# State space block: 192 channels as 128 rows and 64 on both row halves, projections before the running sums, turned x before the small network

## What is computed

```
h      = _ln(x)                                   # 192 channels
zxbcdt = h @ in_proj_w.T                          # z: 384, xBC: 512, dt: 6 columns
xBC    = silu(conv4(xBC) + conv_b)                # xs 384, B 64, C 64
dt     = softplus(dt + dt_bias);  dA = exp(-dt * exp(A_log))
hn     = hprev * dA_t + dtx_t * B_t;  y_t = hn . C_t     # 6 heads of 64, 64 states
y      = rmsnorm((y + D_skip * xs) * silu(z)) * ssm_norm_w
x      = x + y @ out_proj_w.T
f      = _ln(x) @ fc1_w.T                         # 768 columns: a (384) and g (384)
return x + (f_a * silu(f_g)) @ fc2_w.T            # "the small network"
```

## Time and profile before

| what | us |
|---|---|
| median of 3 runs (2194.4 to 2195.69) | 2195.28 |
| the profiled execution | 2192.55 |
| its span | 2190.8 |
| TensorE busy, of the span | 1974.5 (90%) |
| VectorE, ScalarE, GpSimd busy | 1137.2, 750.8, 428.5 |
| first turned rows y of the state space block | 932.84 |
| first `new_state` (start of full turn 0) | 975.01 |
| `new_state` of turns 1, 3, 4 | 1033.52, 1142.61, 1196.30 |
| `new_state` of turn 7 | 1357.98 |
| last write of h in the block | 1405.45 |

### The profile page before, as it was taken

How to read it: one execution, slowest core, us unless ns; L and a number is a source line. 1 busy time by engine, 2 the same in 40 slices (tenths; PEclk the granted TensorE clock), 3 DMA queues, 4 the chain that set the end, 5 groups by cost and what they waited for, 6 DMA issues and landing times. The chain is left out here.

```text
span 2190.8 us, 27883 instructions
## 1 busy us (share of the span) xinstructions
PE 1974.5 (90%) x10040; PEld 1243.3 (57%) x10048; DVE 1137.2 (52%) x2687; ACT 750.8 (34%) x1251; POOL 428.5 (20%) x526
## 2 busy tenths in 40 slices
PE   4996618999999999679999999699999999999997
PEld 2343513444444444446666665465567888888886
DVE  5798577666666756156677676337411222222221
ACT  1434002555455545355555554121111111111111
POOL 5200100121012201211111111110371222322232
PEclk9988558999999999979999999789999999999999
DMA  2600002121111111000000000200123221222221
GB/s 64 229 34 0 0 13 89 47 61 52 51 37 58 51 51 30 13 14 6 6 6 6 6 6 6 97 2 1 48 77 95 67 59 30 67 60 61 67 36 19
DMA packets 68618, 94.30 MB, mean 43 GB/s; under 512 B 15354, under 2 KB 57630, under 8 KB 66209
## 3 DMA queue, kind: packets, MB, share of 16 engines
q1 hardware_dynamic: 52354, 76.76, 10.9%
q0 software_dynamic: 16128, 15.76, 4.1%
HBM read 54.53 MB, written 39.47 MB: 43 GB/s over the span
## 5 line engine op out<-in xcount | busy, mean ns | idle before, releaser
L972 DVE TENSOR_REDUCE row_max<-c_ps_m 128x1 f32<-128x512 f32 x384 | 252.6, 686 | 115.9 <-PE c_ps_m L1130 110.5
L1308 ACT ACTIVATE e<-c_ps_s 128x512 f32<-128x512 f32 x384 | 216.6, 596 | 222.1 <-PE c_ps_s L1146 221.3
L2593 DVE TENSOR_TENSOR e_f<-e_ps_u,e_gate 128x512 f32<-128x512 f32 x120 | 83.0, 691 | 271.2 <-ACT e_gate L2875 178.7
L2394 POOL DMA_INDIRECT out<-m_o,m_row_of x80 | 125.7, 1571 | 281.5 <-issue 251.6
L2810 PE MATMUL e_ps_o<-m_w,e_f 128*128 128x192 f32 x960 | 162.6, 326 | 0.9 <-DVE e_f L2593 0.9
L1130 PE MATMUL c_ps_m<-c_kT,qT 96*128 96x512 bf16 x384 | 150.3, 398 | 11.0 <-DVE row_max L972 10.9
L2810 PEld LDWEIGHTS e_ps_o<-m_w,e_f 128*128 128x128 f32 x960 | 158.1, 190 | 3.3 <-DVE e_f L2593 1.3
L1146 PE MATMUL c_ps_s<-qT,c_kT 97*128 97x512 bf16 x384 | 145.5, 389 | 12.3 <-ACT e L1308 5.0
L2875 ACT ACTIVATE e_gate<-e_ps_g 128x512 f32<-128x512 f32 x120 | 71.6, 597 | 242.3 <-PE e_ps_g L2784 162.3
L2778 PE MATMUL e_ps_g<-m_xT,m_w 128*128 128x256 f32 x480 | 129.6, 392 | 1.0 <-DVE h L2425 1.0
L2778 PE MATMUL e_ps_u<-m_xT,m_w 128*128 128x256 f32 x480 | 123.2, 379 | 0.0
(11 more groups left out here) (430 smaller groups left out, 3766.2 us busy)
## 6 DMA issues: line engine op xcount, KB each, us to landing
dealt<-x SPq DMA_DIRECT2D x8, 1290.0 KB, 15.1
m_x<-dealt SPq DMA_DIRECT2D x40, 258.0 KB, 2.7
spread<-parts SPq DMA_DIRECT2D x24, 384.0 KB, 2.4
qT<-spread SPq DMA_DIRECT2D x144, 64.0 KB, 2.4
c_kT<-spread SPq DMA_DIRECT2D x144, 64.0 KB, 2.4
m_w<-in_w13e SPq DMA_DIRECT2D x8, 1152.0 KB, 5.3
m_w<-in_w2e SPq DMA_DIRECT2D x8, 576.0 KB, 6.4
out<-h SPq DMA_DIRECT2D x8, 384.0 KB, 4.5
```

The costliest lines, as they stand in the source:

```text
L972: dve.tensor_reduce(row_max[:, n // J, n % J:n % J + 1], ps_m[:, n % 2, :], AX_X, ALU.max)\
L1308: act.activation(e[:, n % LIVE_E, :], ps_s[:, n % 2, :], ACT.Exp, scale=QSCALE).then_inc(e_ready, 1)
L2394: pool.indirect_dma_start(out=out_rows, out_offset=bass.IndirectOffsetOnAxis(ap=row_of[:, n % 2, r:r + 1], axis=0), in_=o[:, n % 2, r, :], ...
```

## The change

1. The 192 channels stand as rows 0 to 127, and the last 64 channels twice, on rows 0 to 63 and on rows 64 to 127. For this `y` and `y2` are 256 columns wide; VectorE copies columns 128 to 191 to 192 to 255 after a drain (`tensor_copy`, at the end of `apply_1` and of `apply_2`), and the turned rows are two blocks of 128 rows. The weights `wz`, `wx`, `wf1` and `ln12` are laid out the same way (`halves`).
2. `projections(*keys)` takes the place of `steps`, `project` and `hidden`. It runs the 128-row matmul of each key first, and then the 64-row matmuls of all keys, in turn on the lower and the upper row half.
3. The order of products: dt, x0, x1, z0 ahead of `chunk`; x2, x3, z1, z2 ahead of `running_sums`; turned x 0 and 1 ahead of the small network, 2 and 3 after its first pair. `ssm_order` has the same order, which also changes which product stands five places ahead of which.
4. ScalarE: all three `z_silu` directly after `conv_silu` 0; `conv_silu` 1 to 3 after the squares and ahead of `decay`.
5. VectorE: `times_cb` 0 between `norm_2` and `apply_2`; `times_dt` 0 and 1, `times_cb` 1 and `norm_1` behind `apply_2`; `times_cb` 2 and 3 and `times_c` at the end. The addition of x2 to h goes to GpSimd, and VectorE waits for it (`x2_added`) at `add_out` of the next sequence and at `add_o`.
6. GpSimd: `rstd_1` of t + 2 after two of the four `dtx_rest`. In `apply_1` y is now given free only after both y and xm are written, and copied.

```diff
-        begin(("dt", 0), ("x", 0), ("x", 1), ("x", 2), ("x", 3), ("z", 0), ("sums", 0))
+        begin(("dt", 0), ("x", 0), ("x", 1), ("z", 0), ("x", 2), ("x", 3), ("z", 1), ("z", 2), ("sums", 0))
...
+            def projections(*keys):
+
+                for key in keys:
+                    k, t, i = key
...
+                    free(key)
...
+                        w, col, rows = weights(key)
+                        pe.matmul(bank(key), w[:, 0, col:col + P], rows[:, 0, :], start=True, stop=False)
+                for n, key in enumerate(keys):
+                    half = row_half[n % 2]
...
+                        w, col, rows = weights(key)
+                        last = pe.matmul(bank(key), w[half, 1, col:col + P], rows[half, 1, :], start=False, stop=True)
+                    last.then_inc(w_psum, 1)
...
                     norm_2(t)
+                if begins:
+                    times_cb(u, 0)
+                if ends:
+                    apply_2(t)
...
                     conv_silu(u, 0)
-                    z_silu(u, 0)
+                    for m in range(KD):
+                        z_silu(u, m)
                 if ends:
                     for j in range(J):
                         squares(t, j)
                 if begins:
+                    for i in range(1, 4):
+                        conv_silu(u, i)
                     decay(u)
...
+                    here = kit.h[:, t * J:(t + 1) * J, :]
+                    pool.tensor_tensor(here, here, x2[:, :, :], ALU.add).then_inc(x2_added, 1)
```

More of the change, by code:

```diff
@@ L1715, in apply_2 @@
                 dve.wait_ge(r2_ready, t + 1)
[L1716 to L1720, removed]
+                ln_apply(dve, y2[:, :, 0:C], x2, mv2, rstd2)
+                dve.drain()
+                dve.tensor_copy(y2[:, :, C:2 * P], y2[:, :, P:C]).then_inc(y2_ready, 1)
             def times_gate(t, m):
@@ L1761, in turn @@
                     norm_2(t)
+                if begins:
+                    times_cb(u, 0)
+                if ends:
+                    apply_2(t)
+                if begins:
+                    times_dt(u, 0)
+                    times_dt(u, 1)
+                    times_cb(u, 1)
                 if later:
@@ L1764, in turn @@
                 if ends:
-                    apply_2(t)
-                    add_x2(t)
+                    times_gate(t, 0)
                 if begins:
-                    for j in range(J):
-                        times_cb(u, j)
+                    times_dt(u, 2)
+                    times_dt(u, 3)
+                if later:
+                    apply_1(t + 2)
+                if ends:
+                    times_gate(t, 1)
+                    times_gate(t, 2)
+                if begins:
+                    times_cb(u, 2)
+                    times_cb(u, 3)
                     for j in range(J - 1):
                         times_c(u, j)
[L1772 to L1779, removed]
                 if ends:
@@ L1819, in turn_rows @@
                 for j in range(J):
-                    last = pe.transpose(bank(key)[0:CH, j * P:(j + 1) * P], src[:, j, c * CH:(c + 1) * CH],
-                                        kit.ident[:, :])
+                    last = pe.transpose(bank(key)[:, j * P:(j + 1) * P], src[:, j, c * P:(c + 1) * P], kit.ident[:, :])
                 last.then_inc(w_psum, 1)
[L1824 to L1828, removed]
-                    for c in range(2):
-                        last = pe.matmul(bank(key)[:, j * NH:(j + 1) * NH], yT[:, c, j * P:(j + 1) * P], wz[:, c, DI:ZW],
-                                         start=c == 0, stop=c == 1)
-                last.then_inc(w_psum, 1)
@@ L1834, in project, with weights @@
-            def project(k, t, i):
-                key = (k, t, i)
-                w, m = (wx, XORDER[i]) if k == "x" else (wz, i)
-                free(key)
-                for c in range(2):
-                    last = pe.matmul(bank(key), w[:, c, m * P:(m + 1) * P], yT[:, c, :], start=c == 0, stop=c == 1)
-                last.then_inc(w_psum, 1)
+            row_half = (slice(0, P // 2), slice(P // 2, P))
+            def weights(key):
+                k, t, i = key
+                if k in ("g", "a"):
+                    return wf1, (KD + i if k == "g" else i) * P, y2T
+                return (wx, XORDER[i] * P, yT) if k == "x" else (wz, i * P, yT)
@@ L1965, in output @@
                 last.then_inc(w_psum, 1)
-            def hidden(k, t, m):
-                key = (k, t, m)
-                if k == "g" and m == 0:
-                    pe.wait_ge(by_act["y2"], count("y2", t, 1))
-                free(key)
-                col = (KD + m if k == "g" else m) * P
-                for c in range(2):
-                    last = pe.matmul(bank(key), wf1[:, c, col:col + P], y2T[:, c, :], start=c == 0, stop=c == 1)
-                last.then_inc(w_psum, 1)
             def turn(t):
```

104 lines of the change are left out of this document (55 added, 49 removed).

## The result

The changed kernel takes 2240.94 us (median of 4 runs, 2238.66 to 2243.26); the kernel before, run beside it, takes 2194.84 (2189.66 to 2195.69). The ratio is 1.0216, with a 95% interval of 1.0203 to 1.0229: slower by 46 us. The span of the profiled execution went from 2190.8 to 2240.7.

What follows compares the result with a forecast made beforehand. With TensorE nearly saturated, the new order makes the loop across engines bind: 58.0 us plus 2.0 for the clock a turn. Turns +37.0, prologue +10.7, tail -0.9 on 2192.55, plus 2.7 to the median: 2242 us, 8-in-10 range 2210 to 2265.

Steps and rivals of the forecast that it cites:

- The wait at the sums: In each turn TensorE stands still 4.1 us ahead of the running sums, until ScalarE's silu of z0.
- the band of 2 to 3: In each turn TensorE waits 2 to 3 us ahead of y2.
- Tables: ScalarE's two exposed table switches a turn: only the 1.28 us load counted; the skill page gave some 19 us more.
- The clock: In each full turn, half clock behind TensorE's waits costs 2.0 us, bounds 0 to 5.
- The clock falls twice: Rival: clock falls twice a turn, stays down through the small network, 5 us a turn, 2263 us; chance 0.16.
- the rival at 2228: Rival: the clock stays full through the turns, 14 us less, 2228 us; chance 0.20.
- Work saved: Row halves at 0.48 us a pair cut TensorE's work by 4.2 us a turn, from 52.0 to 47.8.
- dt's halves: Ahead of the end of chunk: dt's halves might run beside x0's, then 0.9 us less.
- stays the bound: Rival: TensorE stays the bound and the kernel gets faster, turns of 49.5 us, 2169 us; chance 0.10.
- The conv silus: ScalarE's silu of conv 3 (0.65), load and decay (about 2.0) now come ahead of the rows, on the loop.
- Prologue and tail: Before the first new_state: sums 4.3 us later, 6.4 more behind them, +10.7 together; tail in turn 7, -0.9.
- The sum: Seven turns +37.0 us, prologue +10.7, tail -0.9: +46.8 on the profiled execution of 2192.55 us.

Runs made afterwards that it cites:

- e2: Changed kernel with x2 in the first group of projections and z0 in the second: 2217.97 us, ratio 1.0116 to the kernel before.
- e3: Changed kernel with VectorE's first times_cb behind apply_2 again: 2226.22 us, ratio 1.0153 to the kernel before.
- e10: Changed kernel with both x2 in the first group instead of z0 and times_cb 0 behind apply_2: 2247.72 us, ratio 1.0037 to the kernel before.
- e4: Changed kernel with unread matmuls filling two TensorE waits, four ahead of the sums and two ahead of y2: 2222.87 us, ratio 1.0128 to the kernel before.
- e5: Changed kernel with all 64-row matmuls on the lower row half: 2295.58 us, ratio 1.033 to the kernel before.
- e9: e8 with the first gate's product and first two dt products ahead of apply_1 on VectorE: 2215.68 us, ratio 0.99 to the kernel before.
- e6: Changed kernel with silus of conv 1 to 3 back behind y2, turned x later, VectorE's times_dt and gates moved along: 2281.71 us, ratio 1.0262.
- e1: Changed kernel with all moves undone, row halves kept in the order of the kernel before: 2191.6 us, ratio 0.9993 to the kernel before.
- e11: Kernel before, 96 + 96 rows and no row halves, with the moves of e8 and e9: 2222.73 us, ratio 0.9925 to the kernel before.
- e8: e1 with z0 in the first group, its silu early, z1 behind the sums, z2 behind y2, y2 ahead of norm_1: 2210.77 us, ratio 0.9948.
- e7: e1 with two unread matmuls filling the wait ahead of the fourth gated group: 2211.07 us, ratio 0.9947 to the kernel before.

## Why the prediction was right, point by point

The steps of turn 3 as forecast and as measured, from the rows of the first section. The forecast column adds up to 58.0 (with rounding) and leaves out the 2.0 for the clock; turn 3, at 61.04, is the longest but the first:

| step | forecast | measured |
|---|---|---|
| new_state to the end of `chunk` | 14.8 | 14.45 |
| `chunk` to sums | 9.6 | 9.78 |
| sums to `add_out` | 7.25 | 8.02 |
| silu of conv 3, load, decay | 2.6 | 2.63 |
| six exponentials, cb | 4.5 | 4.34 |
| times_cb 0, apply_2, copy | 2.6 | 2.51 |
| y2 turned and scaled | 2.1 | 2.84 |
| small network, last gate | 10.4 | 12.37 |
| `o` | 4.0 | 4.10 |

**The two moves that cost.** The wait at the sums was forecast at 4.1 and is 4.17, ended by the silu of z0. The first `times_cb` waits for cb, and TensorE 2.35 for y2, in the band of 2 to 3. e2, e3 and e10 show that both are causes: 3.2 and 1.7 a turn back, 4.9 together, of the 5.4 that a turn lost (59.5 for 54.1).

**Tables.** The last copy ends at 1191.89, the load starts at 1191.91 and ends at 1193.19, and the silu starts at 1193.20: a switch costs its 1.28 and nothing more. The Trainium skill (ScalarE: Activation LUTs, "What ACT_TABLE_LOAD costs") adds a drain of 1.38 to each; this trace doesn't agree, with 0.02 ahead of the load and 0.01 behind it. So the sum was right to go by the rows.

**The clock.** I took 2.0 a turn between 0 and 5; e4 gives 2.3. In turn 3 it costs some 2.9: 0.8 at the sums, 0.7 at y2 and 1.4 in the first pair of the small network. "The clock falls twice" is what happened in most turns, but it didn't stay down through the small network, and so costs 2.9 and not 5. The clock held (the rival at 2228) in none of the seven. I had also read the kernel before too kindly: its first two turns are together 6.5 longer than two of 53.7, but turn 4 (1196.30 to 1251.67, 55.37) is 1.7 too long as well, with a granted clock of 0.97, and the short turn 6 hides it.

**Work saved.** The pairs run at 0.48 as the last layer's rows said, and e5 prices them at 3.5 a turn where I had 4.3. The forecast that TensorE's work falls by 4.2 was too high: in e4, at the full clock, it is busy 54.14, of which the six added products take 5.65, so its own work is 48.5, 3.5 less than before. In the first group dt's halves ran partly beside x0's, which I had left open: the end of `chunk` came 0.35 early. TensorE "stays the bound" was the rival on the faster side, and e9 shows that it was possible with these halves, though not in this order.

**The conv silus.** The 2.6 was right as a step of the loop. To conclude that it could be won back by undoing the move (e6) was wrong: 0.9 came back, and a turn with all of e6's moves was 2.8 longer.

**Prologue and tail.** The total was near, 11.6 for 10.7, but its terms were not. I had the sums 4.3 later and 6.4 more behind them. From the first turned y to the sums it is 20.6 before and 21.4 now, 0.8 more: before, the sixteen records of the x projections took 9.59 there, partly at half clock, and the sums waited for log_a, so z0's wait met existing slack. y itself is turned 1.5 later, behind xm and the copy, which I had costed at nothing. And from sums to the first new_state it is 30.8 for 21.6, 9.2 more: half clock and a slow `apply_1` (2.26) on top of the list that I had. This is read from the rows; no run tested it. The tail gave 1.4 for 0.9.

**The sum.** 37.4 + 11.6 - 1.4 = 47.6 in the block, for 46.8. The span grew by 49.9, because the unchanged part ahead of the block was 2.6 later in this execution. The first turn (63.17) is long as it starts at half clock; the other six are 59.5 in the mean. That the seven turns came out within 0.4 of the forecast is partly luck. By e4 the loop at the full clock is 57.2 and not 58.0, the clock costs 2.3 and not 2.0, and the long first turn, which I hadn't forecast, makes up the rest.

## What to carry to other kernels

When the bounding engine is 97% busy, still add up the loop through the others before taking work off it: here there were 1.7 us of slack, and the halves' gain ran into a wait of 1.9 for the next engine (e1). Group work for one engine's sake only after asking which bank the next product takes, and who reads that bank last: one place in the list, z0 for x2, was worth 3.2 us a turn. And read an in-order queue from its late consumer backwards: moving one gate ahead of work that was not urgent (e9) freed 1.3 to 1.5 us a turn, and no new wait took its place.

## What the runs showed of the hardware

**The wait just ahead doesn't settle the clock.** In e2 each turn has the same wait of 1.75 ahead of the second gated group; `out` behind it took 4.07 in three turns and 4.68 to 5.75 in the other four (behind the first turn, a turn took 56.1 to 56.8 either way):

```profile
1122.11 1.52 PE L1976 MATMUL d_ps_w<-ident,yy 128*128 128x128 f32 x9 [1.75 <-ACT silu_z L2072]
1123.47 4.07 PE L1988 MATMUL d_ps_w<-w_out,yy 128*128 128x192 f32 x24
...
1178.36 1.52 PE L1976 MATMUL d_ps_w<-ident,yy 128*128 128x128 f32 x9 [1.75 <-ACT silu_z L2072]
1179.72 5.75 PE L1988 MATMUL d_ps_w<-w_out,yy 128*128 128x192 f32 x24
```

In e11 the clock fell in a turn without any wait: eight records of projection x at 5.38, for 3.68 in its neighbours, with a granted clock of 0.68 from 1244.14 to 1249.50:

```profile
1086.34 3.68 PE L1839 MATMUL d_ps_w<-d_yT,wx 96*128 96x512 f32 x8
...
1244.14 5.38 PE L1839 MATMUL d_ps_w<-d_yT,wx 96*128 96x512 f32 x8
```

And e8 has a wait of 1.47 in six of its turns, and the granted clock was 1.00 in five of them (0.92 in the first). In the kernel before, the same wait of 1.21 for y2 left turn 3 at 1.00 and turn 4 at 0.97, where the turned rows behind it took 1.83 instead of 1.08. Filling a wait took the falls away at the places where it was tried (e4, e7); why the clock fell in e11 stays open.

**VectorE beside GpSimd.** The normalised y took 1.24 in the full turns of the kernel before. In the changed kernel it takes 2.02 when a product of GpSimd runs beside it:

```profile
1221.50 1.63 POOL L1553 TENSOR_TENSOR dtx_rest<-dtx,to_end 128x384 f32<-128x384 f32 x2 [0.76 <-DVE dtx L1667]
...
1221.80 2.02 DVE L1580 TENSOR_SCALAR d_y<-h,d_mv,d_rstd 128x192 f32<-128x192 f32 x4
```

The second half of `apply_1`, right behind it and with GpSimd idle, took 1.24. e9 moved it beside GpSimd too and it took 2.09, e8 did not and there it took 1.24. In the prologue, beside GpSimd's fills of constants, it took 1.96 in both kernels. What the slowdown costs the kernel was not measured apart.
